# K stored by four transfers, its Toeplitz load and a group's ordering copy one channel later

## The chip, the cores and the metric

The kernel runs on one core of a Trainium2 chip. The metric is the device time of one execution in microseconds (us). Five engines work from their own lists of instructions and meet at semaphores: TensorE (PE), VectorE (DVE), ScalarE (ACT), GpSimd (POOL) and SyncE (SP). Transfers are issued by SyncE, ScalarE and GpSimd, and 16 DMA engines carry them out.

## The reference

The input x has 128 sequences of 64 channels and 1024 steps. Four layers follow each other, each adding its result to x:

```
x = x + L0(x, length)        # long convolution with a kernel K per channel, steps beyond a sequence's length masked
x = x + L1(x, A1, B1, id1)   # low-rank adapter: (x B[id]) A[id], 8 adapters of rank 16
x = x + L2(x, A2, B2, id2)   # the same with 64 adapters
x = x + L3(x, W, bias, id3)  # a 64 x 64 matrix over the channels, by subject
```

K comes from complex exponentials of the parameters, `K = 2 * einsum('hn,hnl->hl', Cs, exp(dtA * l)).real`, 1024 values for each of 64 channels. L1 and L2 mix over the 1024 steps, so the kernel needs their A tables in an order by step as well as by adapter, and products of the two layers' tables with each other.

## The kernel before

The kernel has three stages: a setup, a stage of 64 channels, and a stage of 64 pairs of sequences. The change is in the first two.

**The stage of channels.** One channel h is one convolution of 128 sequences. Its x (512 KB) is loaded by SyncE, turned by eight transposes on PE (L187), split into a high and a low half of 16 bits by ScalarE (`high_x`, L193 and L194; `high_sum`, L200) and VectorE (`low_x`, L209 to L213), and multiplied on PE (L1064, 42 products) with Toeplitz matrices of K. These come from DRAM by two loads of 384 KB, `toep` (L179) from `k_rows` and `diff` (L180) from `d_rows`, into one of U = 4 buffers. A part that two results share is copied from PSUM by ScalarE (`copy_common`, L853) and added by VectorE (L1030); VectorE selects by the mask (L1013, L1034), and ScalarE issues the store of the result, x1, two channels later (`store_x1`, L846).

The channels run in turns of XU = 8 positions u, and each engine has its own body for a turn. PE turns channel h + 1 before it multiplies channel h. SyncE's body for channel h: wait until channel h - 1 is multiplied (`conv_done`), load the Toeplitz pair of channel h + 3, wait until x1 of channel h - 1 is stored, and load x of channel h + 7 into that place.

**K in chunks.** K is made in chunks of eight channels, one per turn, for the next turn. VectorE, ScalarE (`k_trig` at position 0, `k_decay` at positions 5 and 7) and PE make it; at position 4 ScalarE and VectorE split it into `khl` (`k_high`, `k_low`). At position 5 SyncE stores it (`store_k`, L344): for each half of 64 partitions, for `k_rows` and `d_rows`, and for the high and the low part, one transfer, eight in all, in runs of 32 values of 16 bits. SyncE then waits until all have landed, and loads the pair of channel h + 3, the first of the next chunk.

**Groups of adapters.** In four of the turns (1 to 4, of 0 to 7) two groups of eight L2 adapters are prepared, one in positions 0 to 3, one in 4 to 7. SyncE loads a group's B and A tables (L767 and L768, 512 KB each) at position 2 or 6 of the half turn before, once the tables of the group before are used up. At position 0 or 4 ScalarE orders A (L887, the copy from `nat_a` to `by_k`). PE turns B after the channel at position 0 or 4 (`turn_b`, L1111), turns the ordered A at 1 or 5, and joins the tables at 2 or 6; ScalarE and VectorE split the results in between. At position 3 or 7 SyncE stores what came of it, 512 KB and 64 KB (L762, L764).

Semaphore waits stand in each engine's list, so whatever an engine waits for also holds back all that is behind it in its list. SyncE's list is that of the queue q1, ScalarE's stores go by q10, GpSimd's gathers by q0.

Of the kernel before, what the change touches and what calls it, by code (L numbers as in the profile page):

```python
# [7 lines left out]
F16 = mybir.dt.float16  # L8
# [3 lines left out]
ACT = mybir.ActivationFunctionType  # L12

P = 128
B = 128
H = 64
L = 1024
# [10 lines left out]
E = 8  # L28
# [19 lines left out]
def storage(nc, ctx):  # L48
# [3 lines left out]
    def sb(name, shape, dt):  # L52
        return ctx.enter_context(nc.sbuf_tensor(name, shape, dt))
# [46 lines left out]
    m.idf = sb("idf", [P, 4, B], F32)  # L100
    m.g_out = sb("g_out", [P, P], F32)
    m.colf = sb("colf", [P, 4], F32)
    m.khl = sb("khl", [P, 2, KP, TC], F16)
    m.par = sb("par", [P, 4, H + E], F32)
    m.step = sb("step", [P, 2, TC], F32)
    m.k0add = sb("k0add", [P, H // 2], F32)
# [68 lines left out]
def load_toeplitz(m, sp, h, u):  # L175


    row = h * (2 * KPAD)
    sp.dma_start(m.toep[:, u, :, :], bass.AP(m.k_rows.tensor, row + QUARTER, [[1, P], [KPAD, 2], [1, TW]])).then_inc(m.toep_loaded[u], 16)  # L179
    sp.dma_start(m.diff[:, u, :, :, :],  # L180
                 bass.AP(m.d_rows.tensor, h * (2 * L), [[1, P], [HALF, 4], [1, DW]])).then_inc(m.toep_loaded[u], 16)
# [117 lines left out]
def k_bank(m, bank):  # L299

    return m.ps[:, bank, 0:KP * 2 * TC].rearrange("p (q n) -> p q n", n=2 * TC)
# [18 lines left out]
def k_high(nc, m, act, k, bank):  # L320

    act.wait_ge(m.k0_added, k + 1)
    for e in range(2):
        rows = slice(64 * e, 64 * e + 64)
        nc.scalar.activation(m.khl[rows, 0, :, :], k_bank(m, bank)[rows, :, e * TC:e * TC + TC], ACT.Copy).then_inc(m.k_high, 1)


def k_low(nc, m, dve, k, bank):

    dve.wait_ge(m.k_high, 2 * k + 2)  # L330
    for e in range(2):
        rows = slice(64 * e, 64 * e + 64)
        nc.vector.tensor_tensor(m.khl[rows, 1, :, :], k_bank(m, bank)[rows, :, e * TC:e * TC + TC], m.khl[rows, 0, :, :],
                                ALU.subtract).then_inc(m.khl_ready, 1)


def store_k(m, sp, k, halves=(0, 1)):

    sp.wait_ge(m.khl_ready, 2 * k + 2)
    for e in halves:  # L340
        for n, rows in enumerate((m.k_rows, m.d_rows)):
            for part in range(2):
                dst = rows[bass.ds(k * E + e * KP, KP), part, 0:L].rearrange("q (a c) -> a q c", c=TC)
                sp.dma_start(dst, m.khl[64 * e + 32 * n:64 * e + 32 * n + 32, part, :, :]).then_inc(m.k_stored, 16)  # L344


def x1_slot(m, u):
# [23 lines left out]
def setup_stage(nc, m, x, lens, id1, id2, id3, log_dt, C, log_A_real, A_imag, D, A1, B1, bias):  # L371
# [3 lines left out]
    with ExitStack() as ctx:  # L375
# [47 lines left out]
        with nc.Block() as block:  # L423
            @block.sync
            def _(sp):
                sp.dma_start(logs[:, 0:64], log_A_real).then_inc(logs_loaded, 16)
                sp.dma_start(logs[:, 64:65], log_dt.rearrange("(h o) -> h o", o=1)).then_inc(logs_loaded, 16)
                sp.dma_start(aim[:], A_imag).then_inc(aim_loaded, 16)
                sp.dma_start(cri[:], C).then_inc(c_loaded, 16)
                sp.dma_start(nat_a.rearrange("p (a n) -> p a n", a=8), A1.rearrange("a (p k) r -> p a (k r)", k=J)).then_inc(a_loaded, 16)  # L430

                sp.wait_ge(iota_made, 2)
                sp.dma_start(nat_b, B1.rearrange("a r t -> (a r) t")).then_inc(b_loaded, 16)
                for h in range(2):
                    sp.dma_start(x_slot(m, h), x[:, h, :]).then_inc(m.x_loaded[h], 16)
                sp.wait_ge(k0_cleared, 1)
                sp.dma_start(k0add[TC - 1:P:2 * TC, :].rearrange("e (k q) -> e k q", q=KP),
                             D.rearrange("(k e q) -> e k q", e=2, q=KP)).then_inc(d_loaded, 16)
                sp.dma_start(lenc[:], lens.rearrange("(b o) -> b o", o=1)).then_inc(m.ids_loaded, 16)
                for n, v in enumerate((lens, id1, id2, id3)):  # L440
                    sp.dma_start(m.ids[:, n, :], v.rearrange("(o b) -> o b", o=1).broadcast_to([P, B])).then_inc(m.ids_loaded, 16)
                sp.dma_start(m.biases[:], bias.rearrange("s o d -> s (o d)")).then_inc(m.bias_loaded, 16)
                sp.wait_ge(const_made, 4)
                sp.dma_start(m.k_rows[:, :, L:KPAD].rearrange("h s z -> (h s) z"), zeros[:]).then_inc(pad_stored, 16)
                sp.dma_start(m.g_rows[GROW:GROW + R, :], ident[0:R, 0:R]).then_inc(m.g_stored, 16)
                for h in range(2, XU - 1):
                    sp.dma_start(x_slot(m, h), x[:, h, :]).then_inc(m.x_loaded[h], 16)
                store_k(m, sp, 0, (0,))

                sp.wait_ge(m.k_stored, 128)  # L450
                sp.wait_ge(pad_stored, 16)
                sp.wait_ge(a_turned, 1)
                load_toeplitz(m, sp, 0, 0)
# [198 lines left out]
def channel_stage(nc, m, x, W, A2, B2):  # L652
# [9 lines left out]
    with ExitStack() as ctx:  # L662
# [56 lines left out]
        with nc.Block() as block:  # L719
            @block.sync  # L720
            def _(sp):
# [3 lines left out]
                def body(i, first=False, last=False, group=False, next_group=False, make_k=False, start_k=False):  # L725
                    for u in range(XU):
                        h = i * XU + u
                        if not (last and u > U):
                            if not (first and u == 0):

                                sp.wait_ge(conv_done, h)
                            if make_k and u == XU - 3:
                                store_k(m, sp, i + 1)

                                sp.wait_ge(m.k_stored, 128 * (i + 2))
                            if first and u == 0:
                                load_toeplitz(m, sp, 1, 1)
                                load_toeplitz(m, sp, 2, 2)
                                sp.dma_start(group_rows(m)[0:P, :, :], at).then_inc(m.a_stored, 16)
                            load_toeplitz(m, sp, h + 3, (u + 3) % U)  # L740
                        if first and u == 5:

                            sp.wait_ge(m.a1_back, 1)
                            load_group(1)
                        if group and u % U == 2:
                            g = 2 * i - 1 + u // U
                            if next_group or u < U:

                                sp.wait_ge(b_turned, g)
                                sp.wait_ge(a_ordered, g)  # L750
                                load_group(g + 1)
                        if not (last and u):
                            v = (u + XU - 1) % XU
                            if not (first and u == 0):

                                sp.wait_ge(x1_stored[v], 16 * (i + (1 if u else 0)))
                            load_x(h + XU - 1, v)
                        if group and u % U == U - 1:
                            g = 2 * i - 1 + u // U
                            sp.wait_ge(g_out_ready, g + 1)  # L760
                            rows = m.g_rows[0:GROW, :].rearrange("(n a) r -> n a r", n=P)
                            sp.dma_start(rows[:, bass.ds((g - 1) * 8, 8), :], g_out.rearrange("p (a r) -> p a r", r=R)).then_inc(m.g_stored, 16)  # L762

                            sp.dma_start(group_rows(m)[bass.ds(g * P, P), :, :], at).then_inc(m.a_stored, 16)  # L764
# [76 lines left out]
            def _(act):  # L841
# [13 lines left out]
                def body(i, first=False, last=False, group=False, next_group=False, make_k=False, start_k=False):  # L855
                    for u in range(XU):
# [10 lines left out]
                        if make_k and u == 0:  # L867
                            k_trig(nc, m, act, i + 1)
                        if make_k and u == 4:
                            act.wait_ge(m.k_stored, 128 * (i + 1))  # L870
                            k_high(nc, m, act, i + 1, 3)
                        if start_k and u == 5:
                            act.wait_ge(m.tables_ready, i + 2)
                            k_decay(nc, m, i + 2, m.dv, 0, m.decay_v_ready)
                        if start_k and u == 7:
                            k_decay(nc, m, i + 2, m.du, 1, m.decay_u_ready)
                        if first and u == 6:
                            act.wait_ge(m.a1_back, 1)
                            S.activation(a1c[:, 0, :, :], group_turned, ACT.Copy, scale=A_SCALE).then_inc(m.a1_high, 1)
                        if not (first and u == 0):  # L880
                            copy_common(h - 1, first and u < 2)
                        if not (first and u < 2):
                            store_x1(h - 2, (u - 2) % XU)
                        if group and u % U == 0:

                            act.wait_ge(a_loaded, 16 * g)
                            S.activation(by_k.rearrange("p (k a r) -> p k a r", k=J, a=8),  # L887
                                         nat_a.rearrange("p (a k r) -> p k a r", a=8, k=J), ACT.Copy).then_inc(a_ordered, 1)
                        if group and u % U == 1:
                            act.wait_ge(b_turned, g)  # L890
                            S.activation(m.bt[:, bass.ds(g * 8, 8), 0, :, :], by_adapter(group_turned), ACT.Copy).then_inc(b_high, 1)
# [580 lines left out]
```

## Time and profile before

| | |
|---|---|
| runs shown, median (lowest to highest) | 784.6 us (781.02 to 784.93) |
| the profiled execution, its span | 789.68 us, 787.9 us |
| PE, DVE, ACT, POOL busy | 714.3, 576.3, 435.5, 385.2 us |
| chain that ended last | PE 60%, DMA 17%, SyncE's sequencer 5% |
| DMA | 219.96 MB, mean 279 GB/s |
| stage of the channels | from about 36 to 500 us |

Busy time is the sum over an engine's instructions, waits left out. The chain is followed back from the last instruction, at each step to what released it. A window row lists, for one stretch, its length, each engine's busy time with the count of instructions, the granted clock of TensorE as a share of full speed (`PEclk`; 2.4 GHz is full, 1.2 GHz half), the mean busy share of the 16 DMA engines and the rate.

### The profile page before, as it was taken

Reading aid. Unit: us, or ns where it says so; the run is one execution under the profiler, and the core shown is the slowest. Engines: PE = TensorE matmul, PEld = TensorE weight load, DVE = VectorE, ACT = ScalarE, POOL = GpSimd, SP = SyncE. Lnnn points to the kernel's source line nnn. Section 1 sums busy time; section 2 is a strip of 40 time slices with the busy share of each in tenths; the row PEclk is TensorE's granted clock in tenths of the full one; section 3 lists DMA queues with packets and bytes.
Section 4 is the critical chain, followed back from the end, with each engine's and each line's share of the span. In section 5 each row is a group of like instructions: output and inputs, shape, how many; then the busy total and the mean of one; then the engine's idle time right before and its main releaser. Section 6 shows DMA issues by size and latency. Waiting matters only on the chain.

```text
span 787.9 us, 19729 instructions
## 1 busy us (share of the span) xinstructions
PE 714.3 (91%) x6624; PEld 541.5 (69%) x6624; DVE 576.3 (73%) x1116; ACT 435.5 (55%) x760; POOL 385.2 (49%) x680
## 2 busy tenths in 40 slices
PE   2299998979979969999989999499999999999997
PEld 2277776758858847777767777377767777777774
DVE  7677985675856837686766866278888888888885
ACT  5535535545524643553635433157777777777775
POOL 1000188888881000005677700267677676766672
PEclk9599999989989999999999999779999999999999
DMA  6487899788897896989889895579999999999974
GB/s 217 119 283 249 277 303 325 254 306 280 259 345 241 279 318 210 333 253 314 278 297 276 261 349 191 225 244 320 310 300 322 314 310 310 321 317 315 315 269 158
DMA packets 122231, 219.96 MB, mean 279 GB/s; under 512 B 20738, under 2 KB 80706, under 8 KB 122178
## 3 DMA queue, kind: packets, MB, share of 16 engines
q1 hardware_dynamic: 103026, 166.56, 66.3%
q10 hardware_dynamic: 9936, 33.59, 10.9%
q0 software_dynamic: 9216, 19.15, 7.8%
q8 instruction: 27, 0.44, 0.2%
q14 instruction: 26, 0.21, 0.1%
HBM read 146.35 MB, written 72.91 MB: 278 GB/s over the span
## 4 chain that ended last, share of the span: by engine, by line
PE 60%; DMA 17%; SPq 5%; issue 4%; DVE 4%; ACT 3%; POOL 1%; POOLq 1%; ACTq 0%; DVEq 0%
PE ps L1064 23%; PE ps L1385 10%; DMA outt<-in_L_cond_A 9%; PE ps L1372 7%; PE ps L1418 5%; DMA x_rows<-xt 5%; PE ps L187 4%; PE ps L1401 3%; PE ps L1400 3%; SPq L344 2%; DMA d_rows<-khl 2%; PE ps L1391 2%; PE ps L1430 1%; ACT xTh L194 1%; DMA diff<-d_rows 1%
## 5 line engine op out<-in xcount | busy, mean ns | idle before, releaser
L1064 PE MATMUL ps<-toep,xTh 128*128 128x512 f16 (+3 forms) x1024 | 214.4, 305 | 2.5 <-DMA diff<-d_rows 2.2
L1064 PE MATMUL ps<-toep,xTl 128*128 128x512 f16 (+3 forms) x512 | 149.3, 304 | 0.0
L1064 PEld LDWEIGHTS ps<-toep,xTh 128*128 128x128 f16 x1024 | 99.3, 100 | 56.1 <-issue 4.3
L811 POOL DMA_INDIRECT gnow<-g_rows,idx_g x64 | 59.6, 931 | 145.1 <-DMA g_rows<-g_out 118.9
L787 POOL DMA_INDIRECT wnow<-in_L_cond_weights,idx_w x64 | 62.4, 976 | 102.3 <-DVEq L1001 85.3
L1255 POOL DMA_INDIRECT asel<-a_rows,idx_a x64 | 71.8, 1121 | 75.7 <-PE ps L1401 74.1
L1250 POOL COPY bsel<-bt 128x256 f16 x256 | 93.2, 407 | 4.1 <-issue 3.8
L1030 DVE TENSOR_TENSOR ps<-ps,common 128x512 f32<-128x512 f32 x64 | 44.6, 696 | 65.3 <-ACT common L853 65.1
L1340 DVE TENSOR_TENSOR xTl<-ps,xTh 128x1024 f16<-128x1024 f32 x64 | 78.4, 1224 | 12.5 <-ACT xTh L1299 9.2
L1064 PE MATMUL ps<-diff,xTh 128*128 128x256 f16 x512 | 87.3, 273 | 0.0
L853 ACT ACTIVATE common<-ps 128x256 f32<-128x256 f32 x64 | 24.3, 379 | 109.1 <-PE ps L1064 109.1
L210 DVE TENSOR_TENSOR xTl<-ps,xTh 128x1024 f16<-128x1024 f32 x64 | 77.7, 1214 | 0.0
L209 DVE TENSOR_TENSOR xS<-ps,xS 128x256 f32<-128x256 f32 x64 | 26.9, 421 | 64.9 <-ACT xTh L194 64.6
L1299 ACT ACTIVATE xTh<-ps 128x1024 f16<-128x1024 f32 x64 | 65.4, 1021 | 12.0 <-PE ps L1372 11.9
L1064 PE MATMUL ps<-diff,xTl 128*128 128x256 f16 x256 | 69.8, 273 | 0.0
L1064 PEld LDWEIGHTS ps<-toep,xTl 128*128 128x128 f16 x512 | 51.0, 100 | 26.5 <-issue 2.6
L194 ACT ACTIVATE xTh<-ps 128x1024 f16<-128x1024 f32 x64 | 65.2, 1019 | 0.0
L187 PE MATMUL ps<-ident,xt 128*128 128x128 f32 x256 | 37.9, 297 | 26.3 <-DVE xSl L213 16.7
L200 ACT ACTIVATE xSh<-xS 128x256 f16<-128x256 f32 x64 | 26.7, 417 | 52.7 <-DVE xS L209 52.7
L1418 PE MATMUL ps<-bsel,xTh 128*128 128x64 f16 x1024 | 54.6, 195 | 0.0
L1418 PEld LDWEIGHTS ps<-bsel,xTh 128*128 128x128 f16 x1024 | 53.0, 99 | 0.8
L1313 ACT ACTIVATE outt<-ps,bias_t 128x1024 f32<-128x1024 f32 x32 | 35.7, 1115 | 31.2 <-PE ps L1401 31.2
(227 smaller groups left out, 1750.0 us busy)
## 6 DMA issues: line engine op xcount, KB each, us to landing
toep<-k_rows SPq DMA_DIRECT2D x64, 384.0 KB, 6.9
diff<-d_rows SPq DMA_DIRECT2D x64, 384.0 KB, 8.5
xt<-in_x SPq DMA_DIRECT2D x32, 512.0 KB, 4.7
x_rows<-xt ACTq DMA_DIRECT2D x32, 512.0 KB, 5.5
xt<-x_rows SPq DMA_DIRECT2D x32, 512.0 KB, 7.2
out_dram<-outt SPq DMA_DIRECT2D x32, 512.0 KB
out_dram<-diff SPq DMA_DIRECT2D x32, 512.0 KB
toep<-x_rows SPq DMA_DIRECT2D x24, 512.0 KB, 6.6
```

The source lines that it names most:

```text
L187: last = nc.tensor.transpose(m.turned[:, j, :], x_slot(m, u)[:, j * P:(j + 1) * P], m.ident[:])
L194: nc.scalar.activation(m.xTh[:, u % 2, :, :], m.turned, ACT.Copy).then_inc(m.xTh_ready, 1)
L210: V.tensor_tensor(m.xTl[:, u % 2, :, :], m.turned, m.xTh[:, u % 2, :, :], ALU.subtract).then_inc(m.xTl_ready, 1)
L787: gp.indirect_dma_start(m.wnow[:, v, :], None, w_src, bass.IndirectOffsetOnAxis(ap=m.idx_w[:, q:q + 1], axis=0)).then_inc(w_gathered[v // ...
L811: gp.indirect_dma_start(m.gnow[:, v, :], None, m.g_rows, bass.IndirectOffsetOnAxis(ap=m.idx_g[0:64, q:q + 1], axis=0)).then_inc(g_gathered ...
L1064: last = PE.matmul(out, xs[x_part], rhs(part), start=start and k == 0, stop=stop and k == 2)
L1250: GP.tensor_copy(m.bsel[:, u % 2, n, :, :, :].rearrange("p s j r -> p (s j r)"), table[:, bass.ds(ids[n], 1), :, :, :].rearrange("p o s j ...
L1255: gp.indirect_dma_start(m.asel[:, p % U, :], None, m.a_rows, bass.IndirectOffsetOnAxis(ap=m.idx_a[:, p:p + 1], axis=0)).then_inc(a_gathere ...
L1299: S.activation(m.xTh[:, u % 2, :, :], psT, ACT.Copy).then_inc(x1Th_ready, 1)
L1340: V.tensor_tensor(m.xTl[:, u % 2, :, :], psT, m.xTh[:, u % 2, :, :], ALU.subtract).then_inc(x1Tl_ready, 1)
L1385: PE.matmul(o, w[:, bass.ds(p, 1), :].rearrange("p o d -> p (o d)"), xp[:, u % U, cut], start=(k == 0), stop=False)
L1418: done = PE.matmul(psZ, xT[:, u % 2, j, :], m.bsel[:, u % 2, :, b, j, :], start=(j == 0 and k == 0), stop=(j == J - 1 and k == 2))
```

## The change

`khl` is laid out as [partition, channel, part, 32] where it was [partition, part, channel, 32], so that one transfer can take the high and the low part: `store_k` issues four transfers for eight, and the counts waited for on `k_stored` are halved. SyncE no longer waits for them at position 5, nor does it load a Toeplitz pair there; at position 6 it waits for them and loads two pairs, first that of channel h + 2 (the first of the next chunk), then that of h + 3. ScalarE orders A at position 1 or 5 instead of 0 or 4, behind the split of x and ahead of the common copy; the eight decays of position 5 move to position 6.

```diff
-    m.khl = sb("khl", [P, 2, KP, TC], F16)
+    m.khl = sb("khl", [P, KP, 2, TC], F16)
...
     for e in halves:
         for n, rows in enumerate((m.k_rows, m.d_rows)):
-            for part in range(2):
-                dst = rows[bass.ds(k * E + e * KP, KP), part, 0:L].rearrange("q (a c) -> a q c", c=TC)
-                sp.dma_start(dst, m.khl[64 * e + 32 * n:64 * e + 32 * n + 32, part, :, :]).then_inc(m.k_stored, 16)
+            dst = rows.rearrange("h s t -> (h s) t")[bass.ds(2 * (k * E + e * KP), 2 * KP), 0:L].rearrange("m (a c) -> a m c", c=TC)
+            src = m.khl[64 * e + 32 * n:64 * e + 32 * n + 32, :, :, :].rearrange("a q s c -> a (q s) c")
+            sp.dma_start(dst, src).then_inc(m.k_stored, 16)
...
                             if make_k and u == XU - 3:
                                 store_k(m, sp, i + 1)
-
-                                sp.wait_ge(m.k_stored, 128 * (i + 2))
+                            if make_k and u == XU - 2:
+
+                                sp.wait_ge(m.k_stored, 64 * (i + 2))
+                                load_toeplitz(m, sp, h + 2, (u + 2) % U)
...
-                            load_toeplitz(m, sp, h + 3, (u + 3) % U)
+                            if not (make_k and u == XU - 3):
+                                load_toeplitz(m, sp, h + 3, (u + 3) % U)
...
-                        if start_k and u == 5:
+                        if start_k and u == 6:
                             act.wait_ge(m.tables_ready, i + 2)
                             k_decay(nc, m, i + 2, m.dv, 0, m.decay_v_ready)
...
+                        if group and u % U == 1:
+
+                            act.wait_ge(a_loaded, 16 * g)
+                            S.activation(by_k.rearrange("p (k a r) -> p k a r", k=J, a=8),
+                                         nat_a.rearrange("p (a k r) -> p k a r", a=8, k=J), ACT.Copy).then_inc(a_ordered, 1)
                         if not (first and u == 0):
                             copy_common(h - 1, first and u < 2)
                         if not (first and u < 2):
                             store_x1(h - 2, (u - 2) % XU)
-                        if group and u % U == 0:
-
-                            act.wait_ge(a_loaded, 16 * g)
-                            S.activation(by_k.rearrange("p (k a r) -> p k a r", k=J, a=8),
-                                         nat_a.rearrange("p (a k r) -> p k a r", a=8, k=J), ACT.Copy).then_inc(a_ordered, 1)
```

## Rows read from the trace of the kernel before

**Rows 1.** Windows by turn: length, busy times (counts), PEclk, DMA share, GB/s

```profile
97.00:157.80 60.80, 57.48 (x488) 45.98 (x486) 42.33 (x67) 28.36 (x60) 51.46 (x53) 0.97 0.90 296
157.80:222.10 64.30, 59.03 (x488) 46.25 (x488) 43.98 (x69) 30.92 (x64) 55.15 (x57) 0.95 0.87 288
222.10:287.00 64.90, 59.02 (x489) 46.25 (x488) 42.64 (x69) 30.99 (x64) 16.46 (x17) 0.95 0.88 280
287.00:353.90 66.90, 58.21 (x490) 46.09 (x491) 44.73 (x76) 32.52 (x67) 0.00 (x0) 0.95 0.87 279
353.90:407.60 53.70, 51.52 (x411) 39.34 (x410) 37.31 (x65) 24.76 (x56) 34.46 (x41) 0.97 0.89 290
407.60:457.70 50.10, 49.82 (x410) 38.68 (x409) 36.17 (x62) 22.00 (x51) 32.51 (x40) 1.00 0.93 287
```

**Rows 2.** Windows of two half turns, and of the stage of pairs

```profile
97.00:125.40 28.40, 28.38 (x248) 22.63 (x246) 20.10 (x32) 11.48 (x21) 24.02 (x26) 1.00 0.96 325
...
259.10:287.00 27.90, 27.70 (x240) 21.96 (x240) 18.01 (x30) 14.36 (x35) 0.00 (x0) 1.00 0.91 267
...
530.00:780.00 250.00, 248.34 (x2820) 178.04 (x2818) 211.33 (x422) 188.40 (x239) 172.69 (x418) 1.00 0.92 303
```

**Rows 3.** Waits: who for whom, us in total, times, longest

```profile
ACT outt L887 <- DMA outt<-in_L_cond_A: 31.3, 7, 9.5
...
PE ps L187 <- DVE xSl L213: 16.7, 5, 5.4
...
PE ps L1111 <- DMA bsel<-in_L_cond_B: 2.8, 2, 1.8
```

**Rows 4.** The chain in order of time: start, us, what

```profile
270.67 4.17 DMA d_rows<-khl
...
279.02 11.82 DMA outt<-in_L_cond_A
...
297.18 6.11 PE ps L1064 x42
...
476.83 5.22 PE ps L1064 x42
482.93 5.22 PE ps L1064 x42
```

**Rows 5.** Timeline of ScalarE: start, us, line, count, idle time before it

```profile
123.25 1.06 ACT L887 ACTIVATE outt<-outt 128x1024 f32<-128x1024 f32 x1 [3.55 <-DMA outt<-in_L_cond_A]
...
253.86 1.06 ACT L887 ACTIVATE outt<-outt 128x1024 f32<-128x1024 f32 x1 [0.45 <-DMA outt<-in_L_cond_A]
...
266.51 0.39 ACT L853 ACTIVATE common<-ps 128x256 f32<-128x256 f32 x1 [2.55 <-PE ps L1064]
...
290.86 1.06 ACT L887 ACTIVATE outt<-outt 128x1024 f32<-128x1024 f32 x1 [9.55 <-DMA outt<-in_L_cond_A]
```

**Rows 6.** Timeline of SyncE's issues in the third group turn

```profile
265.35 1.42 SPq L344 DMA_DIRECT2D k_rows<-khl  x2
...
275.61 0.47 SPq L180 DMA_DIRECT2D diff<-d_rows  x1
```

**Rows 7.** Issue to landing, 97 to 354: the x1 stores (L846), then diff (L180)

```profile
DMA to landing us min/median/max: 3.3/6.1/8.6
...
DMA to landing us min/median/max: 6.3/8.3/9.9
```

**Rows 8.** The page's groups of instructions: busy, mean ns, idle before

```profile
L1030 DVE TENSOR_TENSOR ps<-ps,common 128x512 f32<-128x512 f32 x64 | 44.6, 696 | 65.3 <-ACT common L853 65.1
...
L210 DVE TENSOR_TENSOR xTl<-ps,xTh 128x1024 f16<-128x1024 f32 x64 | 77.7, 1214 | 0.0
```

**Rows 9.** The chain in order of time, in the fifth turn

```profile
379.39 3.44 DMA x_rows<-xt
...
394.69 5.78 DMA diff<-d_rows
...
400.51 7.08 PE ps L1064 x42
```

More of the change, by code:

```diff
@@ L324, in k_high @@
         rows = slice(64 * e, 64 * e + 64)
-        nc.scalar.activation(m.khl[rows, 0, :, :], k_bank(m, bank)[rows, :, e * TC:e * TC + TC], ACT.Copy).then_inc(m.k_high, 1)
+        nc.scalar.activation(m.khl[rows, :, 0, :], k_bank(m, bank)[rows, :, e * TC:e * TC + TC], ACT.Copy).then_inc(m.k_high, 1)
 def k_low(nc, m, dve, k, bank):
@@ L332, in k_low @@
         rows = slice(64 * e, 64 * e + 64)
-        nc.vector.tensor_tensor(m.khl[rows, 1, :, :], k_bank(m, bank)[rows, :, e * TC:e * TC + TC], m.khl[rows, 0, :, :],
+        nc.vector.tensor_tensor(m.khl[rows, :, 1, :], k_bank(m, bank)[rows, :, e * TC:e * TC + TC], m.khl[rows, :, 0, :],
                                 ALU.subtract).then_inc(m.khl_ready, 1)
@@ L448, in _ @@
                 store_k(m, sp, 0, (0,))
-                sp.wait_ge(m.k_stored, 128)
+                sp.wait_ge(m.k_stored, 64)
                 sp.wait_ge(pad_stored, 16)
@@ L869, in body @@
                         if make_k and u == 4:
-                            act.wait_ge(m.k_stored, 128 * (i + 1))
+                            act.wait_ge(m.k_stored, 64 * (i + 1))
                             k_high(nc, m, act, i + 1, 3)
-                        if start_k and u == 5:
+                        if start_k and u == 6:
                             act.wait_ge(m.tables_ready, i + 2)
```

## The prediction

> **What bounds the kernel now.** I read the page's slices and its chain first: PE holds 60% of the chain, DMA 17%. Then I cut the stage of the channels into its turns of eight channels [rows 1]. A turn with adapter groups (the four stretches from 97.0 to 353.9) takes 60.80, 64.30, 64.90 and 66.90 us, together 256.90, while PE is busy for 57.5 to 59.0 of each. Two half turns run without a wait that matters, 28.40 us for channels 9 to 12 and 27.90 us for channels 29 to 32 [rows 2]. So a group turn that waits for nothing takes 56.30 us, four take 225.2, and **31.7 us** of the stage are waits and what follows from them.
>
> Which wait it is stands in the list of waits [rows 3]: ScalarE's ordering copy (L887) stood 31.3 us, seven times, up to 9.5, for the load of the natural A table. PE's own wait looks smaller and has another name (L187 for VectorE's xSl, 16.7 us), because it is the same one passed on. The chain in order of time shows how, in the third group turn [rows 4]: SyncE issues eight stores of K and, from 270.67, stands 4.17 us until they have landed; then it issues Toeplitz loads, B and A; A lands after 11.82 us, at 290.8; only then come the copy and the next channel's split and transpose. Channel 32 had ended at 287.0, and channel 33's products start at 297.18. They run at half clock at first: 6.11 us for 42 products, 5.22 for the same 42 late in the stage. The granted clock of the three turns with such a wait at their start is 0.95 [rows 1].
>
> ScalarE's rows [rows 5] show that one of a turn's two copies is the expensive one: 9.55 us of waiting at channel 32 (position 0 of a turn), 0.45 at channel 28 (position 4; 3.55 in the first group turn). The position-0 load is the one issued behind the stores of K.
>
> **The change part by part.** I count from the end of channel 28's products (position 4), 259.1 [rows 2]. Before, SyncE issued K's stores from 265.35 on, the second half of the Toeplitz pair for the next chunk's first channel at 275.61 [rows 6] (the first 0.6 earlier), and A at 279.02: 16.5 and 19.9 after the mark.
>
> 1. *Four stores of K in place of eight.* Eight issues took 5.3 us (265.35 to 270.67), so four save some 2.7 us of SyncE in this turn. They still write the same 64-byte runs, so I leave their landing as it was. ScalarE and VectorE write khl with the same counts at another stride: 0, bounds plus or minus 0.1 us a turn. In the setup SyncE and ScalarE issue two fewer each, but there PE waits for the end of the block: 0, at best 0.9.
>
> 2. *The wait for them leaves position 5.* SyncE goes on to its x load. For that it waits for the x1 store of channel 28, which ScalarE issues when channel 29 is through (266.5, 7.4 after the mark [rows 5]) and which takes 6.1 us at the median [rows 7]. So position 6 begins at 7.4 + 0.2 + 6.1 + 0.6 = 14.3. K's stores were all issued near 9.5 and should have landed: the wait, now here, costs nothing; not covered, it is the earlier 4.17 us. Queued behind it on SyncE are two Toeplitz pairs, B, A and the next x load; PE, and ScalarE's copy, wait for those.
>
> 3. *The next chunk's Toeplitz pair one position later.* It is issued at 14.3 and 14.9, against 15.9 and 16.5, but with the x load now ahead of it. Its second half lands 8.3 us later at the median, 9.9 at the longest [rows 7]: 23.2 to 24.8. Channel 32 can start near 22.6 (its end at 27.9 less 5.3). So this edit alone brings a new wait of 0.6 us, at the longest 2.2, in every turn; its lower end is 0, since before it came in time with less.
> The Trainium skill speaks against this move: by "DMA: Bandwidth & Descriptors", Queues, rings and completion order, each DMA engine takes a queue's descriptors in ring order, so the pair would have to let the 512 KB of x through first. No run here shows that for this pair; at the 325 GB/s of [rows 2] it is an estimated 1.6 us, and the sum would be some 6 us worse over four turns.
>
> 4. *A and B.* They follow the second pair: A at 17.3 instead of 19.9. With 11.82 us it lands at 29.1 instead of 31.7. B landed about 2 us ahead of it (PE's longest wait for B is 1.8 us [rows 3], from 287.0), so now near 27, just before PE asks for it at 27.9.
>
> 5. *The ordering copy one position later.* At position 5 A has some 6 us to spare (the wait at position 4 was 0.45 [rows 5]), so those waits go whole. At position 1, channel 33's split is already done when ScalarE stands for A. Queued behind it are the copy of channel 32's common part, the x1 store of channel 31 and the high half of B. A at 29.1, 1.06 for the copy and 0.4 for the common copy end at 30.6 instead of 28.3. VectorE follows with an addition of 0.70 and a selection as long, the low half of B and channel 34's split, each 1.21 as the row of that shape, and two small steps [rows 8], by 35.4 with its gaps; PE wants that near 35.9. So it is hidden with 0.5 us to spare, and each microsecond that A is later costs PE about one. *The eight decays* move to position 6, beside 5.2 us of products, where ScalarE idled 2.55 us before the common copy [rows 5]: 0, bounds plus or minus 0.5 a turn.
>
> What is late next is thus the Toeplitz pair, then B, then the rate of the DMA engines. Their busy time per group turn is share by length [rows 1]: 54.7, 55.9, 57.1 and 58.2 us, together 225.9, as much as PE's 225.2. The highest share of a half turn was 0.96, at 325 GB/s [rows 2]; at 0.96 four turns take 235.3. From PE alone, with 0.6 to 0.9 us for the pair, they take about 228.5. I take the middle, 58.0 a turn or 232.0: **24.9 us** gained, bounds 31.7 (no wait left) and 11.4 (share 0.92, that of the last stage [rows 2]).
> The skill would decide otherwise: the same page's Specifications give a core about 358 GB/s of its memory. By that the 18.5 MB of a turn (288 GB/s by 64.3 us) would be an estimated 52 us, the DMA engines would not bind, and the gain would be the whole 31.7; the trace has 0.96 busy at 325 GB/s and differs, and I go by the trace.
>
> 6. *The turns without groups.* In the one that ends at 407.6 the pair's second half was issued at 394.69 behind the stores, channel 48 stood until 400.5, and its 42 products took 7.08 instead of 5.22 us [rows 9]. Now: channel 44 ended at 379.3, a channel takes 6.10 (482.93 less 476.83 [rows 4]), so channel 45's end is 385.4; 0.2 for the issue, 3.3 to 6.1 for the store [rows 7] and 1.2 for x and the first half put the second half at 390.1 to 392.9, landing 5.8 (as at 394.69) to 8.3 later. Channel 48 could start at 398.4. The gain is 0 to 3.6 (down to the next turn's 50.10 [rows 1]); I take **2.7**. The next such turn has little to give: 0, bounds plus or minus 0.5. In the first turn the group's load now goes ahead of the pair for channel 8, which VectorE holds back anyway: 0, at worst 1.8 lost.
>
> **Sum.** 24.9 + 2.7 = 27.6 us off the profiled execution's 789.7 (span 787.9 and 1.8 around it): 762.1. The median of the runs shown is 784.6, 5.1 lower; some of that must be less waiting, so I give the median a gain of 25: **760 us**.
>
> **Rivals.**
> - *The DMA engines become the bound.* For it: busy time equal to PE's, and 0.92 over the 250 us of the last stage. Against: 0.96 over a half turn. At 0.92 the gain is 11.4 and nothing in the turn without groups: 773 us, and 766 to 777 for the case.
> - *Every wait gone* (A, B and the pair all in time): 31.7 + 3.6 off, 749 us.
> - *SyncE stays as late as it was*, paced by each channel's x1 store (6.1, up to 8.6 us) and not by K's stores: A lands where it did, the position-1 copy holds back the common copy and the x1 store behind it. Against it: the splits are no longer behind the copy. Only the waits at position 4 go (0.45 to 3.55 each [rows 5], some 6 of the 31.3), less the 0.6 to 0.9 a turn of item 3: some 781 us.
> - *Slower: the next chunk's pair lands late.* It stands behind the x1 wait and the x load now, and PE has nothing else to do then. Its price is the lateness and 0.9 to 1.9 us at half clock [rows 4, 9], six times (four group turns, two others). To eat 27.6 and lose 4 more it must cost 5.3 each time: landing 3.4 to 4.4 us after PE asks, over 11 us after its issue in a group turn. The longest of that stretch is 9.9 [rows 7]. Then about 789.
>
> **How the numbers follow.** Forecast (gain of 18 to 32) 0.62; the DMA bound 0.22; every wait gone 0.04; SyncE as late as before 0.06; slower 0.06. What a measurement of this kernel can tell from no change is about 0.5%, 3.9 us. Faster holds the first three: 0.88; same 0.06; slower 0.06. The range 750 to 773 leaves out the last two cases, the edge of every wait gone and the slow end of the DMA bound.
>
> **What would show it.** Right: L887's wait for A falls from 31.3 to under 10 us and costs PE nothing; SyncE no longer stands for the landing of K's stores; the group turns take 57 to 60 us at a DMA share of 0.93 or more, at a granted clock above 0.95; PE waits a little for diff at the first channel of a turn. Wrong: PE waiting over 2 us there in every turn (item 3), L1111 waiting for B (item 4), or A landing again 30 us and more after the mark (item 2). The stage of the pairs after it should keep its time.

## The result and the profile after

The changed kernel takes 759.24 us in the median of four runs (753.52 to 761.12), the kernel before 783.05 beside it: a ratio of 0.9684, 95% interval 0.9620 to 0.9749. A second measurement gave 757.83 us and 0.9661 (0.9621 to 0.9700). The profiled execution takes 757.39 us, span 755.6, which is 32.3 us less than the profiled one before. Medians here are over all runs, while ratios and intervals leave out runs that fell in a slower state of the chip.

The windows by turn of the changed kernel, cut at the ends of channels 8, 16, 24, 32, 40, 48 and 56 as in [rows 1], with the same columns:

```profile
97.20:156.00 58.80, 56.46 (x490) 44.72 (x489) 48.17 (x72) 29.95 (x63) 49.84 (x52) 1.00 0.92 307
156.00:212.50 56.50, 56.02 (x490) 44.83 (x489) 43.33 (x69) 30.79 (x64) 48.35 (x49) 1.00 0.97 325
212.50:268.40 55.90, 55.90 (x490) 44.94 (x489) 42.16 (x69) 30.99 (x64) 23.95 (x25) 1.00 0.96 332
268.40:324.70 56.30, 56.04 (x490) 44.87 (x489) 40.97 (x69) 30.79 (x64) 0.00 (x0) 1.00 0.96 318
324.70:377.10 52.40, 49.76 (x410) 38.60 (x409) 37.08 (x65) 24.79 (x56) 32.31 (x39) 1.00 0.94 302
377.10:426.80 49.70, 49.70 (x411) 38.75 (x410) 36.21 (x62) 22.00 (x52) 33.66 (x41) 1.00 0.94 295
```

The four group turns take 227.5 us instead of 256.9, and PE is busy for 224.4 of them: 29.4 us are gone, nearly the whole 31.7. The granted clock is at 1.00 where it was 0.95 to 0.97. The turn after them gives 1.3, the next one 0.4; the stage of pairs, from the last channel's end at 468.6, takes 287.0 instead of 288.4.

The changed kernel's waits (as in [rows 3]; L886 is the ordering copy, L1067 PE's products):

```profile
ACT outt L886 <- DMA outt<-in_L_cond_A: 14.9, 6, 5.0
...
PE ps L1067 <- DMA diff<-d_rows: 4.5, 3, 2.6
...
PE ps L187 <- DVE xSl L213: 2.6, 4, 1.4
```

ScalarE still stands 14.9 us for A. But PE's wait for the split that stood behind it has fallen from 16.7 to 2.6 us, and its wait for the second half of the Toeplitz pair has grown from one of 2.2 us to three, 4.5 us together. ScalarE's rows at the third group turn's end (as in [rows 5]) show why the longest wait, 5.02 us, is harmless:

```profile
263.17 0.38 ACT L193 ACTIVATE xS<-ps 128x256 f32<-128x256 f32 x1 [0.49 <-PE ps L187]
263.45 1.02 ACT L194 ACTIVATE xTh<-ps 128x1024 f16<-128x1024 f32 x1
265.04 0.42 ACT L200 ACTIVATE xSh<-xS 128x256 f16<-128x256 f32 x1 [0.57 <-DVE xS L209]
270.48 1.06 ACT L886 ACTIVATE outt<-outt 128x1024 f32<-128x1024 f32 x1 [5.02 <-DMA outt<-in_L_cond_A]
```

ScalarE's part of channel 33's split is done at 265.5, VectorE's at 266.5. The wait for A begins after it, so channel 33 multiplies from 269.9 on, while ScalarE still stands.

SyncE's issues of the same turn (as in [rows 6]); the mark, channel 28's end, is here at 240.9:

```profile
247.80 0.50 SPq L344 DMA_DIRECT2D d_rows<-khl  x1
...
254.99 0.42 SPq L179 DMA_DIRECT2D toep<-k_rows  x1
255.60 0.38 SPq L180 DMA_DIRECT2D diff<-d_rows  x1
...
258.54 0.37 SPq L771 DMA_DIRECT2D outt<-in_L_cond_A  x1
```

The pair goes out 14.1 us after the mark (14.3 was forecast), A 17.6 (17.3), and A lands at 270.5, 29.6 after it (29.1). In the two group turns before, A went out 19.6 and 18.4 us after the end of the channel at position 4 and landed 31.3 and 29.0 after it.

### The profile page after: what moved, and what is told of

Read it like the earlier page. It is cut to its first block, busy times and chain, and to the rows that moved or that the text cites. A ratio compares the mean times of both kernels' runs of the same rounds, so it can differ in the third digit from the quotient of the medians.

```text
span 755.6 us, 19659 instructions
## 1 busy us (share of the span) xinstructions
PE 702.8 (93%) x6624; PEld 534.9 (71%) x6624; DVE 577.6 (76%) x1116; ACT 434.6 (58%) x760; POOL 381.0 (50%) x680
## 4 chain that ended last, share of the span: by engine, by line
PE 74%; DMA 10%; DVE 4%; issue 2%; ACT 2%; SPq 2%; POOL 0%; POOLq 0%; ACTq 0%; DVEq 0%
PE ps L1067 31%; PE ps L1388 11%; PE ps L1375 7%; PE ps L1421 6%; PE ps L187 5%; PE ps L1404 3%; PE ps L1403 3%; DMA diff<-d_rows 3%; PE ps L1394 2%; DMA x_rows<-x1h 2%; DMA d_rows<-khl 2%; DMA outt<-in_L_cond_A 2%; DMA x_rows<-xt 1%; PE ps L1433 1%; PE ps L1148 1%
## 5 line engine op out<-in xcount | busy, mean ns | idle before, releaser
L1067 PE MATMUL ps<-toep,xTh 128*128 128x512 f16 (+3 forms) x1024 | 209.7, 300 | 4.5 <-DMA diff<-d_rows 4.5
L1067 PE MATMUL ps<-toep,xTl 128*128 128x512 f16 (+3 forms) x512 | 147.1, 300 | 0.0
L1067 PEld LDWEIGHTS ps<-toep,xTh 128*128 128x128 f16 x1024 | 97.5, 98 | 56.2 <-DMA diff<-d_rows 5.2
L1067 PE MATMUL ps<-diff,xTh 128*128 128x256 f16 x512 | 87.3, 273 | 0.0
L1067 PE MATMUL ps<-diff,xTl 128*128 128x256 f16 x256 | 69.8, 273 | 0.0
L1067 PEld LDWEIGHTS ps<-toep,xTl 128*128 128x128 f16 x512 | 50.2, 98 | 25.1 <-issue 0.4
L1421 PE MATMUL ps<-bsel,xTl 128*128 128x64 f16 x512 | 52.5, 195 | 0.0
L1067 PEld LDWEIGHTS ps<-diff,xTh 128*128 128x128 f16 x512 | 47.4, 98 | 4.3
```

The costliest lines, as they stand in the source:

```text
L1067: last = PE.matmul(out, xs[x_part], rhs(part), start=start and k == 0, stop=stop and k == 2)
L1421: done = PE.matmul(psZ, xT[:, u % 2, j, :], m.bsel[:, u % 2, :, b, j, :], start=(j == 0 and k == 0), stop=(j == J - 1 and k == 2))
```

## The experiments

**The copy alone.** The first four runs take the change apart. My theory was that the gain comes from ScalarE's list: the wait for A no longer stands ahead of a split. The rival was that it comes from SyncE's: K's stores made A late.

```diff
-                        if start_k and u == 5:
+                        if start_k and u == 6:
...
+                        if group and u % U == 1:
...
                         if not (first and u == 0):
                             copy_common(h - 1, first and u < 2)
                         if not (first and u < 2):
                             store_x1(h - 2, (u - 2) % XU)
-                        if group and u % U == 0:
...
```

> The kernel before with the ordering copy at position 1 and 5 and the decays at position 6, and nothing else: eight stores of K, the wait and the Toeplitz pair at position 5. My theory (the gain is that the copy's wait for A no longer stands ahead of the next channel's split): A lands as late as before, B too, so PE loses about 2 us a turn to B and to the common copy, where it lost 6 to 8 and half clock behind it; 761 to 765 us, most of the gain. The rival (the stores of K are what made A late, and their move brings the gain): A is as late as before and holds the common copy and the x1 store behind it; 773 to 779 us.

Measured: 761.6 us, ratio 0.9672 (0.9632 to 0.9712). The copy alone (with the decays' move, which the last run below prices) gives as much as the whole change, within the intervals. Its group turns, cut at channels 8, 16, 24, 32 and 40:

```profile
97.50:154.70 57.20, 56.30 (x491) 44.82 (x489) 45.78 (x71) 29.98 (x63) 48.77 (x51) 1.00 0.95 314
154.70:211.80 57.10, 56.28 (x489) 44.59 (x486) 45.27 (x72) 30.81 (x64) 48.66 (x51) 1.00 0.97 327
211.80:271.70 59.90, 57.78 (x488) 46.05 (x488) 43.25 (x69) 31.00 (x64) 24.27 (x26) 0.97 0.95 307
271.70:328.60 56.90, 56.05 (x490) 45.08 (x491) 41.21 (x69) 30.83 (x64) 0.00 (x0) 1.00 0.95 325
```

They take 231.1 us with A issued about 20 us after the mark, as before. The third turn is 3 us longer than its neighbours. A lands at 215.3 there, 3.5 us after channel 24 has ended, but what PE stands for is B:

```profile
213.88 1.42 PE L1111 MATMUL ps<-ident,bsel 128*128 128x128 f32 x8 [2.08 <-DMA bsel<-in_L_cond_B]
```

Behind that wait the transposes ran slower too, and 5.00 us lay between the products of channels 24 and 25, where 1.58 is usual. Channel 26, which the late copy could have held back, came on time (1.58). In all, PE waits 3.0 us for B in this kernel and 2.6 for the Toeplitz pair; in the changed kernel nothing for B and 4.5 for the pair.

**The stores and the moved wait, without the copy's move.** The changed kernel with the copy and the decays back:

```diff
-                        if start_k and u == 6:
+                        if start_k and u == 5:
...
-                        if group and u % U == 1:
...
                             store_x1(h - 2, (u - 2) % XU)
+                        if group and u % U == 0:
...
```

> The changed kernel with the ordering copy back at position 0 and 4 and the decays back at position 5: four stores of K, the wait and the pair one position later. My theory: A lands some 2.6 us earlier in the turns whose copy waited 7.4 to 9.6 us, which leaves 5 to 7 us of each wait, and the late pair takes a part back; 772 to 777 us. The rival (the stores bring the gain): 762 to 766 us, and the wait of the copy at position 0 below 3 us.

Measured: 782.9 us, ratio 0.9943 (0.9908 to 0.9979). A gain of some 0.6%, under what I expected and far from the rival's. In its profile A lands 1.0 to 1.4 us after the channel at position 0 has ended, where it was 1.8 to 3.9 before, and so the splits at channels 17, 25 and 33 are nearly as late as before (7.2 to 7.5 us between the products of two channels, 7.9 to 10.0 before, 1.58 without a wait).

**Four stores, nothing moved.**

```diff
...
-            for part in range(2):
-                dst = rows[bass.ds(k * E + e * KP, KP), part, 0:L]...
...
+            dst = rows.rearrange("h s t -> (h s) t")[bass.ds(2 * (k * E + e * KP), 2 * KP), 0:L]...
...
```

> The kernel before with four stores of K in place of eight, and nothing else: SyncE still waits for their landing at position 5 and loads the pair there. By my accounting the moved wait is worth nothing beside this, since SyncE must wait for the x1 store of the channel at position 4 in any case, so A goes out as early as with the wait moved, and the pair goes out earlier: within 3 us of the kernel that has four stores and the moved wait, 770 to 776 us. If instead the wait for the landing is what costs, this gives a fifth of that at most: 779 to 783 us.

Measured: 778.11 us, ratio 0.9870 (0.9823 to 0.9917). The time lies between my two ranges, and the accounting failed: I had this kernel within 3 us of the one with the moved wait, and it is 4.8 us below it. The two intervals just overlap, so that the moved wait costs something here is likely and not shown. SyncE's wait for the landing did not shrink with four stores, it grew (32.3 us in all, 24.8 before), which leaves the four issues less a turn as what saves.

**Eight stores, the wait and the pair moved.**

```diff
                                 store_k(m, sp, i + 1)
+                            if make_k and u == XU - 2:

                                 sp.wait_ge(m.k_stored, 128 * (i + 2))
+                                load_toeplitz(m, sp, h + 2, (u + 2) % U)
...
-                            load_toeplitz(m, sp, h + 3, (u + 3) % U)
+                            if not (make_k and u == XU - 3):
+                                load_toeplitz(m, sp, h + 3, (u + 3) % U)
```

> The kernel before with eight stores, but the wait and the Toeplitz pair moved to position 6, and nothing else. By my accounting as good as four stores with the moved wait, as the stores are out before the x1 store has landed: 772 to 778 us. If the issues are what costs (about 0.7 us each), some 3 us slower than that one: 776 to 781 us.

Measured: 785.6 us, ratio 0.9971 (0.9938 to 1.0005): no gain that can be told from none, and both my figures were too low. Of the change's parts on SyncE's side, fewer issues gain about 1% by themselves, and the moved wait with the pair behind it does not.

**The changed kernel beside three others.** The next four ran together, the first as their measure.

> The changed kernel once more, as the measure for the others of this call: 3.2% below the kernel before, near 760 us.

Measured: 757.83 us, 0.9661 (0.9621 to 0.9700). The first of the others puts the wait and the pair back:

```diff
-                            if make_k and u == XU - 2:
-                                sp.wait_ge(m.k_stored, 64 * (i + 2))
-                                load_toeplitz(m, sp, h + 2, (u + 2) % U)
+                                sp.wait_ge(m.k_stored, 64 * (i + 2))
...
-                            if not (make_k and u == XU - 3):
-                                load_toeplitz(m, sp, h + 3, (u + 3) % U)
+                            load_toeplitz(m, sp, h + 3, (u + 3) % U)
```

> The changed kernel with SyncE's wait for K and the Toeplitz pair back at position 5; the copy at position 1 and 5, the decays and the four stores stay. My theory after the first four runs: the moved wait gives nothing and only makes the pair late (channels 16 and 48 began 2.5 and 2.8 us late in the changed kernel's profile), so this is 2 to 5 us faster than the changed kernel, 755 to 758 us. The rival (the freed SyncE brings A and B earlier, and that pays): 2 to 5 us slower, 762 to 765 us, with B late at PE.

Measured: 756.3 us, 0.9636 (0.9598 to 0.9674), six runs of 755.68 to 757.8 beside six of 756.92 to 760.34. If the moved wait does anything here, it costs 1.5 us, less than the 2 to 5 I expected; the rival's loss is not there.

**The stores earlier.** The four stores go to position 4, the wait and the pair to position 5:

```diff
                             if make_k and u == XU - 3:
-                                store_k(m, sp, i + 1)
-                            if make_k and u == XU - 2:

                                 sp.wait_ge(m.k_stored, 64 * (i + 2))
-                                load_toeplitz(m, sp, h + 2, (u + 2) % U)
...
-                            if not (make_k and u == XU - 3):
-                                load_toeplitz(m, sp, h + 3, (u + 3) % U)
+                            load_toeplitz(m, sp, h + 3, (u + 3) % U)
+                            if make_k and u == XU - 4:
+                                store_k(m, sp, i + 1)
```

> The changed kernel with the four stores of K issued at position 4, behind that position's Toeplitz loads and ahead of its wait for an x1 store, and the wait for them and the pair at position 5. The stores then land while SyncE waits for x1 anyway, so if the pair's lateness is what the moved wait costs, the pair is out some 5 us earlier than in the changed kernel, PE no longer waits for diff at the first channel of a turn, and A goes out no later: 750 to 756 us. The rival (the x1 store's landing paces SyncE, and PE's floor is reached): the same as the changed kernel within 2 us.

Measured: 752.78 us, 0.9593 (0.9555 to 0.9632), all six runs (752.05 to 755.58) below all of the changed kernel and of the version above beside it: this one beats both. Its turns without groups, which the change had left with waits, and the group turn that is still long:

```profile
154.30:212.20 57.90, 56.13 (x490) 44.83 (x489) 47.18 (x72) 30.56 (x64) 49.50 (x51) 1.00 0.99 329
...
324.00:373.70 49.70, 49.70 (x411) 38.72 (x409) 36.81 (x65) 24.77 (x57) 30.99 (x37) 1.00 0.91 303
373.70:423.30 49.60, 49.60 (x410) 38.63 (x409) 36.11 (x62) 21.98 (x51) 34.51 (x42) 1.00 0.99 303
```

In the turns without groups PE never stands; no wait of PE for diff is left in its list. In the long group turn PE waits 1.8 us for a split that VectorE has late, which I did not follow further.

**More bytes.** Is the DMA rate the next bound?

```diff
...
                             load_x(h + XU - 1, v)
+                            if u % U == 0:
+                                if not (first and u == 0):
+                                    sp.wait_ge(extra_loaded, 16 * (2 * i + u // U))
+                                sp.dma_start(extra[:], x[:, bass.ds(h, 1), :]...).then_inc(extra_loaded, 16)
...
```

> The changed kernel with two more loads of 512 KB in each turn, of x into a tile that nothing reads: 5 to 6% more bytes in a group turn, whose DMA share is 0.96 to 0.97 already. If PE is the bound there and the share only says that the DMA engines are kept busy: at most 3 us slower, 760 to 763 us. If the DMA rate has become the bound (my second case): 3 us for each of four group turns and 1 to 2 for the others, 772 to 778 us.

Measured: 768.74 us, 0.9795 (0.9754 to 0.9836), 10.9 us more than the changed kernel beside it: between the two figures. Its turns, cut at channels 8, 16, 24, 32, 40 and 48:

```profile
96.60:158.20 61.60, 58.17 (x491) 45.33 (x490) 48.59 (x73) 29.65 (x64) 52.24 (x54) 0.97 0.93 307
158.20:215.70 57.50, 56.01 (x489) 44.56 (x486) 43.54 (x69) 30.75 (x64) 49.42 (x53) 1.00 0.99 336
215.70:273.20 57.50, 56.33 (x491) 45.10 (x491) 42.69 (x70) 30.98 (x64) 20.74 (x21) 1.00 1.01 341
273.20:329.80 56.60, 56.00 (x490) 44.78 (x489) 40.64 (x69) 30.30 (x64) 0.00 (x0) 1.00 0.98 336
329.80:386.50 56.70, 52.17 (x410) 39.49 (x409) 37.50 (x65) 24.80 (x57) 35.12 (x42) 0.94 0.96 306
```

Three group turns carry 5 to 6% more bytes in 0.3 to 1.6 us more time, at up to 341 GB/s. What is lost is lost in the first group turn and the one without groups, where the pair comes later still (PE waits 8.2 us for diff in all) and the granted clock falls to 0.97 and 0.94. So the mean rate was not yet the bound of the other group turns; what costs is the lateness of a few loads. Whether the bytes made the pair late, or the two more issues ahead of it in SyncE's list, this run does not tell apart.

**One copy moved, the other not.** I had read in [rows 5] that the position-0 copy is the expensive one. The kernel before, with the copy at position 1 for a turn's first group alone (and the decays at position 6, which the cut leaves out):

```diff
...
+                        if group and u == 1:
+
+                            act.wait_ge(a_loaded, 16 * g)
...
                             store_x1(h - 2, (u - 2) % XU)
-                        if group and u % U == 0:
+                        if group and u == 4:
```

> The kernel before with the copy moved to position 1 for a turn's first group alone; the second group's copy stays at position 4, the decays go to position 6, the stores of K stay as before. By my reading of ScalarE's rows the position-0 copy is the expensive one (25 of 31 us of waiting): four fifths of what both moves gave (3.3%), so 764 to 768 us against 786. The rival (once the first wait is gone the second grows, since A then goes out later against the channels): half of it or less, 772 us and more, with the position-4 waits above 3 us each.

Measured: 772.25 us, ratio 0.9834 (0.9778 to 0.9890): half of the gain, as the rival had it, though only two of the four position-4 waits are above 3 us (1.4, 4.4, 2.2 and 3.6). Its waits of PE for K's split, of ScalarE at position 4 (L892) and at position 1 (L883):

```profile
PE ps L1116 <- DVE khl L333: 11.6, 4, 4.2
...
ACT outt L892 <- DMA outt<-in_L_cond_A: 11.6, 4, 4.4
...
ACT outt L883 <- DMA outt<-in_L_cond_A: 4.6, 2, 4.2
```

Position 4 now costs what position 0 had hidden. There the copy stands ahead of a split, VectorE makes the low half of K only after that split, and PE's transposes of B wait for it (4.17 us at the longest).

**The decays back.**

```diff
-                        if start_k and u == 6:
+                        if start_k and u == 5:
```

> The changed kernel with the eight decays back at position 5, so that the ordering copy stands behind them there. If the move of the decays is only room for the copy: the same within 2 us (757 to 761 us), as A has some 6 us to spare at position 5. The rival: 3 us of decays ahead of the copy and the common copy make VectorE's additions and the x1 store late in every group turn: 762 to 768 us.

Measured: 759.1 us, 0.9689 (0.9644 to 0.9733), the changed kernel's ratio (0.9684 and 0.9661): no effect of the decays' place is seen.

## Why the prediction was right, and where its steps were not

*The bound and the sum.* 760 us was forecast, 759.24 measured. Taking a group turn without waits as the floor held: 56.30 us from two half turns, 55.9 to 56.5 reached in three of four.

*Item 5, the copy, was the change.* Alone it gives 0.9672; all the rest without it gives 0.9943. The pricing of its slack held roughly: in the changed kernel A landed 2.1 us after channel 32's end, 0.9 later than the forecast's 29.1 against 27.9, and 2.03 us lay between the products of channels 33 and 34 instead of 1.58, where 0.5 to spare and then one for one would give 0.4; with the copy alone, A 1.8 us behind channel 16's end cost 0.65 before channel 18, where the pricing gives next to nothing. But the prediction never said how much each part was worth alone, and its third rival shows that it had this wrong: A as late as before, with the copy moved, was priced at some 781 us, and the copy alone, with A issued about as late as before, took 761.6. What A's and B's earlier issue adds beside the copy cannot be told from nothing (0.9672 without, 0.9684 and 0.9661 with; the intervals leave room for some 5 us).

*The signs.* L887's wait was to fall below 10 us and fell to 14.9, nearly all of it at position 1, where it costs PE almost nothing; the sign asked for too much. SyncE's standing for K's stores did go, from 24.8 us in eight waits to 3.7 in three. Three of the four group turns were shorter than the 57 to 60 forecast. A landing 30 us and more after the mark, a sign of being wrong, came in the first group turn (31.3) and cost nothing there, as channel 16 was late for the pair by then.

*What bounds the kernel, the sentence on the two copies, was wrong.* The position-4 wait of 0.45 us was small because the stall at position 0 had given that load its time. With that stall gone it took half the gain away; only moving both copies works.

*Item 2, "costs nothing", held; what came late was the x1 store ahead of it.* In the turn without groups the chain of the changed kernel, as in [rows 9], names K's stores:

```profile
350.14 3.86 DMA x_rows<-xt
357.00 6.94 DMA d_rows<-khl
364.71 6.96 DMA diff<-d_rows
371.72 5.40 PE ps L1067 x42
```

The chain goes by what landed last, and that was 0.3 us after something else. SyncE's own waits between 345 and 370 us show what it stood for before the pair, the x1 store of channel 44:

```profile
SPq L723 <- DMA x_rows<-x1h: 5.6, 1, 5.6
SPq L179 <- DMA d_rows<-khl: 0.3, 1, 0.3
```

ScalarE issued that store at 356.24, and it had landed when SyncE's list went on at 363.19: 6.9 us. *Item 6* had put 3.3 to 6.1 us there, and that term was mis-sized; the wait for K's stores added 0.3. Channel 48 started 2.8 us late instead of 2.3, so the stand is not shorter, and the turn gave 1.3 us and not 2.7. What it did give is the half clock that followed the stand before the change and not this one (5.40 us for the 42 products, not 7.08). Why a stand of 2.3 us was followed by half clock and one of 2.8 was not stays open, and so this 1.3 is luck. The kernel with the stores one position earlier, and the pair again ahead of that x1 wait, needs 49.70 us for the turn.

*Item 3, the late pair,* came as forecast in kind: PE stood 4.5 us for it, three times, up to 2.6, rather than 0.6 in every turn. At channel 16, in the first group turn, it was the x1 store again, 7.9 us from issue to landing in the chain. The prediction set beside it a rule of the Trainium skill ("DMA: Bandwidth & Descriptors", Queues, rings and completion order), by which a queue's descriptors are consumed in ring order and the x load would put the pair back by an estimated 1.6 us. No run here shows that by itself.

*The DMA term was mis-sized.* I took 58.0 us a turn, halfway to a bound by the 0.96 share; the turns took 56.9 on average. The step that failed is the division of a fixed busy time by a highest share. Length by share, the four group turns kept the DMA engines busy for 225.9 us before and 216.6 after, and length by rate they moved the same, 73.4 and 72.9 MB. Nor is the share a ceiling: 1.01 at 341 GB/s in the kernel with more bytes. The Specifications of the Trainium skill's page "DMA: Bandwidth & Descriptors", with about 358 GB/s and so the whole 31.7, came nearer to what was measured.

*How near the number came is partly luck.* The gain of the group turns was 29.4, not 24.9; the smaller gain elsewhere and a median that fell less than the profiled execution (24 us against 32.3) brought the sum back to the forecast.

## What to carry to other kernels

When an engine's list holds a wait for a load ahead of work that the critical engine needs soon, move the wait behind that work before making the load earlier: here the order was worth 25 us, and the earlier loads beside it nothing that could be told from none. A wait that looks cheap may be paid for by another one, so move all of a kind together or measure them apart. A wait that is moved later takes its dependants with it, here behind an x1 store; put the transfer earlier instead, where the queue waits anyway (5 us here). Read a chain's last releaser beside the engine's own list of waits: another one may have ended 0.3 us before it.

## What the runs showed of the hardware beyond expectation

The mean busy share of the 16 DMA engines went to 1.01 over 57.5 us at 341 GB/s, so a share of 0.96 does not mean that the rate is used up. Nor does a transfer cost a fixed busy time: the four group turns moved about the same bytes with 225.9 us of it before the change and 216.6 after. The landing of the same 64-byte runs took 4.17 us after the last issue in one place and 6.94 in another, with other transfers in flight.
